# Transposed group totals ahead of matrix products on TensorE, and a later place for some gate products

## The reference, cut to what matters

```
u, gate = split(x @ W_in.T)                 # 2 x 2048 channels
u     = silu(causal_conv4(u) + conv_b)
dt, B, C = split(u @ Wx.T)                  # 64, 16, 16; each rms-normed
delta = softplus(dt @ Wdt.T + dt_bias)
state = exp(delta*A) * state + (delta*u) * B          # for each of 16 states, over time
y     = sum over states of state * C, + u * D_param
x1    = layernorm(x + (y * silu(gate)) @ W_out.T)
out   = layernorm(x1 + x1 @ W.T + b + the LoRA product of the best rank)
```

## Time and profile before

| | |
|---|---|
| median of 3 runs (range) | 2567.99 us (2561.28 to 2569.66) |
| the profiled execution | 2566.21 us, span 2564.4 us |
| PE busy | 2198.9 us, 86% |
| DVE busy | 2140.0 us, 83% |
| POOL busy | 1797.0 us, 70% |
| ACT busy | 1473.6 us, 57% |
| mean granted clock of PE | 0.92 |
| DMA | 353.52 MB, mean 138 GB/s |

### The profile page before, as it was taken

How to read it: one execution, slowest core, us unless ns; L and a number is a source line. 1 busy time by engine, 2 the same in 40 slices (tenths; PEclk the granted TensorE clock), 3 DMA queues, 4 the chain that set the end, 5 groups by cost and what they waited for, 6 DMA issues and landing times.

```text
span 2564.4 us, 30651 instructions
## 1 busy us (share of the span) xinstructions
PE 2198.9 (86%) x10528; PEld 1600.0 (62%) x10528; DVE 2140.0 (83%) x2551; ACT 1473.6 (57%) x2083; POOL 1797.0 (70%) x768
## 2 busy tenths in 40 slices
PE   6988679788879969899979979899979995988977
PEld 5766557577645547687855547677866563765545
DVE  3448789999999499889989789999989789999831
ACT  3368757576655265666675445665675456555421
POOL 3368989888598378777668666877678687678600
PEclk9999889998879979999989989999989996988988
DMA  4265556465223325755542323555453331352213
GB/s 158 63 214 199 185 175 211 151 203 178 78 70 102 104 77 175 253 187 189 169 132 85 103 62 127 187 192 185 156 161 105 103 95 56 131 169 79 78 50 115
DMA packets 152651, 353.52 MB, mean 138 GB/s; under 512 B 17776, under 2 KB 27376, under 8 KB 152496
## 3 DMA queue, kind: packets, MB, share of 16 engines
q1 hardware_dynamic: 152496, 351.56, 42.9%
HBM read 282.65 MB, written 68.85 MB: 137 GB/s over the span
## 4 chain that ended last, share of the span: by engine, by line
PE 54%; DVE 29%; issue 8%; ACT 5%; POOL 3%; DMA 1%; SPq 0%; DVEq 0%; POOLq 0%; ACTq 0%
PE bank L717 15%; DVE drive L796 13%; PE state_t L670 12%; PE bank L694 7%; PE bank L696 7%; PE bank L695 7%; DVE y_acc L811 6%; PE bank L670 3%; DVE scratch L818 2%; PE bank L752 2%; DVE ln_stats L882 1%; POOL drive L1176 1%; ACT decay L1022 1%; ACT L1022 1%; DVE dt_slot L844 1%
## 5 line engine op out<-in xcount | busy, mean ns | idle before, releaser
L1176 POOL TENSOR_TENSOR drive<-delta_u,b_bcast 128x2048 f32<-128x2048 f32 x256 | 1170.7, 4576 | 281.0 <-PE state_t L670 280.3
L796 DVE TENSOR_TENSOR_SCAN drive<-decay,drive 128x512 f32<-128x512 f32 x1024 | 1195.9, 1206 | 53.1 <-POOL drive L1176 33.4
L1022 ACT ACTIVATE decay<-delta,a_sb 128x512 f32<-128x512 f32 x1024 | 693.8, 687 | 397.9 <-DVE drive L796 393.9
L670 PE MATMUL state_t<-identity,drive 128*128 128x128 f32 x4096 | 639.4, 297 | 223.1 <-DVE drive L796 139.0
L670 PEld LDWEIGHTS state_t<-identity,drive 128*128 128x128 f32 x4096 | 514.8, 152 | 438.9 <-DVE drive L796 186.9
L694 PE MATMUL bank<-cols_high,w_split 128*128 128x512 f32 (+1 forms) x1312 | 562.7, 429 | 38.5 <-POOL w_split L1202 37.5
L811 DVE SCALAR_TENSOR_TENSOR y_acc<-state_t,c_rows,y_acc 128x512 f32<-128x512 f32 x720 | 514.9, 737 | 70.3 <-PE state_t L670 65.2
L696 PE MATMUL bank<-cols_high,w_split 128*128 128x512 f32 (+1 forms) x1312 | 526.6, 401 | 0.0
L695 PE MATMUL bank<-cols_low,w_split 128*128 128x512 f32 (+1 forms) x1312 | 524.9, 400 | 0.0
L717 PE MATMUL bank<-channels,w_raw 128*128 128x512 f32 x1024 | 476.5, 596 | 4.6 <-POOL channels L1198 4.6
L1182 POOL TENSOR_TENSOR y_acc<-y_acc,scaled 128x512 f32<-128x512 f32 x240 | 309.7, 1290 | 77.8 <-ACT scaled L1036 77.7
(11 more groups left out here) (92 smaller groups left out, 1396.2 us busy)
## 6 DMA issues: line engine op xcount, KB each, us to landing
w_split<-w_split SPq DMA_DIRECT2D x288, 512.0 KB, 3.7
b_bcast<-b_rows SPq DMA_DIRECT2D x256, 256.0 KB, 3.4
w_raw<-in_w_out SPq DMA_DIRECT2D x128, 256.0 KB, 2.9
w_raw<-in_w_in SPq DMA_DIRECT2D x96, 256.0 KB, 3.5
gates<-scratch SPq DMA_DIRECT2D x64, 256.0 KB, 3.7
scratch<-gates SPq DMA_DIRECT2D x64, 256.0 KB, 4.6
w_raw<-in_x_cols SPq DMA_DIRECT2D x32, 256.0 KB, 3.6
rows<-in_x_rows SPq DMA_DIRECT2D x4, 2048.0 KB, 9.1
```

The lines of the kernel that those rows point to most:

```text
L670: last = engine.transpose(bank[0:tile.shape[1], i * P:(i + 1) * P], tile, identity[:, :])
L796: engine.tensor_tensor_scan(state, decay[(GT * s + t) % DECAYS][:, :], state, 0.0, ALU.mult, ALU.add).then_inc(signal["scan"])
L1022: engine.activation(decay[i % DECAYS][:, :], delta[:, g % 2, t, :], ACT.Exp, scale=a_sb[:, j, n:n + 1]).then_inc(signal["decay"])
L1176: engine.tensor_tensor(drive[key % DRIVES][:, :, :], du[:, :, :], row, ALU.mult).then_inc(signal["drive"])
```

## The change

Two edits to the planning, none to the instructions themselves. The due of `y_turn` is lowered by `TURN_FIRST`, as that of `turn` is. And the number of gate jobs that are listed between the u jobs of the next sequence is no longer `GATES_BEFORE` but `GATES_BEFORE - GATES_LAST`; the last `GATES_LAST` of them are listed after the first two delta jobs (the line that does so, L354, was there and served sequence 0 alone). Between the u jobs of sequences 0 to 3 there were 0, 12, 12 and 8 gate jobs, and now there are 0, 12, 6 and 0. After the delta jobs there were 4, 0, 0 and 0, and now there are 4, 0, 6 and 4. For sequence 3 four more (4 to 7) go from the list of `beside(2)` to the head of that of `beside(3)`, ahead of the out products.

```diff
-GATES_BEFORE = (4, 12, 12, 8)
+GATES_BEFORE = (4, 12, 12, 4)
+
+GATES_LAST = (4, 0, 6, 4)
...
-        put("PE", due, 0.45, "y_turn", key, [("add", (last, tt)) for tt in range(ADDED)] + [("sum", last)],
+        put("PE", due - TURN_FIRST, 0.45, "y_turn", key, [("add", (last, tt)) for tt in range(ADDED)] + [("sum", last)],
             take=[("bank", ("y_turn", key))])
...
-            gates = GATES_BEFORE[b + 1] if b >= 0 else 0
+            gates = GATES_BEFORE[b + 1] - GATES_LAST[b + 1]
```

## The result

| | before | after |
|---|---|---|
| median (range, runs) | 2564.64 us (2552.38 to 2569.66, 4) | 2468.64 us (2466.84 to 2483.21, 4) |
| ratio, 95% interval | | 0.9645 [0.9594, 0.9696] |
| span of the profiled execution | 2564.4 us | 2466.1 us |

96 us came where 63 were forecast: 2469 us lies 34 under the forecast and 9 under the low end of the range. The direction was right and the size was not.

What follows compares the result with a forecast made beforehand. DVE was taken as the bound most of the time, its idle time as what could be won. 55 + 9 + 2 - 3 = 63 us off the profiled 2566.2 gave 2503 us, range 2478 to 2556.

Steps and rivals of the forecast that it cites:

- the 2 us named: First group's end in sequences 1 to 3: first transpose of `y_acc` within some 2 us of the last sum.
- the clock rule: Out products broken up by turns: pauses halve PE's clock, costing up to 18 us; nothing was charged.
- rival D: Out products hold the banks, y_turns don't get through, 34 us come back: 2532 us; chance 0.07.
- the 7.8 that I left: DVE's waits for L863's transposes outside the three holes, `y_turn` waiting for a bank: 7.8 us expected to remain.
- rival B: Matrix chain takes over: the next sequence starts when it did, so the scans' lead is mostly lost: 2550 us; chance 0.17.
- 55 + 4.6 + 2 = 61.6 us: Gains: 55 from sequences 1 and 2's holes, 4.6 from turns in the last sequence, 2 at other groups' ends.
- The factor 0.93: Sequences 1 and 2: DVE turns only 93% of the returned 36.1 + 22.9 us into work, giving 55 us.
- 525.3 of 564 us: Sequence 1 without the holes: DVE's busy time stays 525.3 us in a stretch of 564 us, 93%.
- 4.6 us were counted as won: Last sequence: the wait of 4.63 us for the last y_gate was to go.
- 3 as lost to uncovered gates: Behind sequence 1's out products: four gates of sequence 2 take 21.8 us, 18.6 covered by PE's pause, 3 not.
- rival C: Gates behind the out products delay `x1_turn` because PE's pause closes: 2577 to 2604, say 2590 us; chance 0.10.
- the first term of the sum: DVE holes at the first group's end in sequences 1 and 2: (36.1 + 22.9) x 0.93 = 55 us won.

Runs made afterwards that it cites:

- y_only: The kernel after with the old gate places, so only the lower due of `y_turn` against the kernel before: 2491.4 us, ratio 0.9734.
- y_gates2: Lower due of `y_turn`, six gates of sequence 2 behind its deltas, sequence 3's gates as in the kernel before: 2497.2 us, ratio 0.9747.
- y_gates3: Lower due of `y_turn`, sequence 3's gates moved as in the change, sequence 2's as in the kernel before: 2498.6 us, ratio 0.9757.
- after_again: The kernel after, unchanged, run once more for a second profile: 2470.2 us, ratio 0.9654 to the kernel before.
- gates_only: The kernel after with the old due of `y_turn`, so only the gates moved against the kernel before: 2529.7 us, ratio 0.9888.
- before_again: The kernel before, unchanged, run once more for a second profile: 2561.1 us over 11 runs.
- y_gates_66_00: The kernel after with no gates between the u jobs of sequences 2 and 3, six of sequence 2 behind its deltas: 2490.7 us, ratio 0.9720.
- 8_4: The kernel after, but sequence 3 keeps four gates between its u jobs and four behind its deltas: 2491.1 us, ratio 0.9720.
- 8_8: The kernel after, but all eight early gates of sequence 3 follow its deltas: 2480.4 us, ratio 0.9685.
- drive_in_4: The kernel after with each POOL drive of 128x2048 issued as four of 128x512: 2512.51 us, ratio 0.9831.

## Why the prediction was off

**What held.** The holes were where the rows of before had them and went whole: lags of 0.8, 0.2 and 0.7 us, within the 2 us named. The out products of sequence 0 take 162 us and not 144, 18 more where 17 were worked out. The granted clock in them is 1.00, so charging nothing for the clock rule was right: the turns did not make products dearer. The y_turns got their bank (rival D fell): what DVE waits for them in the whole span, once 22.5 us in 12 waits, is now

```profile
  PE bank L672: 7.5, 7
```

against the 7.8 that I left. The gates were needed as an enabling step: without them at both handovers the time is 21 to 28 us longer by medians (y_only, y_gates2 and y_gates3 against after_again), rival B in part. In the kernel after the chain is early by a few us: POOL's last product for sequence 2's first drive ends at 1260.2, and that drive starts at 1264.4, released by turns of sequence 1.

**What failed, by the terms of the sum.** I count from the first scan of sequence 1 on, with the two profiles of each kernel averaged. Sequences 1 to 3 became 46.3, 33.2 and 12.9 us shorter, 92.4 in all, and the rest of the span 3.4 longer: 89.0 where the sum had 63.

- *The idle time returned.* Of the sum 55 + 4.6 + 2 = 61.6 us are time of DVE in the three sequences; its idle time there fell by 73.6 (166.3 to 92.7), by sequence 39, 27 and 7.5. The stretches of four units that hold the holes went from 37.5, 25.4 and 18.4 us of idle time to 1.1, 0.0 and 1.4. The rest of sequences 1 and 2 became 4 us less idle, that of sequence 3 9.5 more, spread over it; the sum had put only 4.6 us on its hole, and 7.5 came. The factor 0.93, by which DVE was to lose part of the first two holes, was wrong: 66 us came where they had 59. gates_only shows that the gates, which I priced at nothing beside enabling, can give something of their own: 31 us, with 14 us less of lag (88.7 before, 74.9 with it). 12 us too little.
- *The term that wasn't there.* DVE's busy time in the three sequences fell by 18.8 us, which I held constant (525.3 of 564 us). This is the largest error. Some 15 us of it are small instructions that wait for POOL inside their own duration. Over their shortest, counted from 0.45 us, these take 49.4 and 52.8 us in the two profiles of before and 35.7 and 36.3 in those of after. In the first profile of before scans and adds also show 2 ns longer each, 3.3 us over the whole span; the second doesn't show it.
- *Behind the last scan.* 4.6 us were counted as won, PE's wait for the last `y_gate`, and 3 as lost to uncovered gates. The wait is still there:

```profile
2332.07 8.08 PE L719 MATMUL bank<-channels,w_raw 128*128 128x512 f32 x12 [4.23 <-POOL channels L1200]
```

The transposes ahead of it were hardly late before (a lag of 0.1 us), so there was nothing in this wait for a lower due to win. The rest behind the last scan has 11 matmuls more than before and is 3.4 us longer. The 3 us were charged for another place, gates of sequence 2; in the last sequence, where nothing was charged, the cover was gone (rival C's mechanism) and `x1_turn` ends 272 us behind the first scan and not 265. That 3 and 3.4 agree is luck. In all 5 us too much.

63 + 12 + 18.8 - 5 = 89, within rounding. The spans differ by 98.3 because the first scan of sequence 1 also came 9.3 us earlier in this pair of executions. That part isn't of the change: all engines have the same lists up to the first group's end of sequence 1, and before_again shows 718.2 us. The medians over more runs differ by 91, those of the result by 96.

The failed step is thus the first term of the sum, 55 us, worked out with DVE's busy time as a constant and with 0.93 of the holes returned. In its place DVE's busy time fell by 18.8 us and its idle time by 12 more than counted. No rival covers it. Whether the waits on POOL fell for a reason or by chance of alignment I can only argue: 35.7 and 36.3 us repeat within one kernel, and over the variants they go up to 60 us with no order in the edits (59.7 in y_gates_66_00, 51.6 in 8_4, 45.0 in 8_8, 38.6 in y_gates3, 47.7 in gates_only). Each edit shifts where small instructions fall on drives. Of the 21 us between 8_4 and the change, 16 are of this kind. In such a kernel a difference of 10 us between two schedules need not come from what the edit was for.

## What to carry to other kernels

A piece that is ready and gates the next unit of the bound engine needs a due that says so: at three places 2 us of transposes held DVE for 74 us in all. A lead won in one stage is kept only if the chain into every following stage is early too; parts of a change are tested together and alone, since here neither half of the gates' move gained anything without the other. And a forecast that holds an engine's busy time fixed while its instructions shift against another engine's leaves out a term, here 19 us.

## What the runs showed of the hardware

Some small DVE instructions whose operands all lie in SBUF wait inside their recorded duration while POOL works. In the kernels before and after, those that took over 0.3 us more than the shortest of their kind (37 and 35) each ended at most 0.42 us behind the end of a POOL instruction. In the kernel before, POOL's drive and DVE's L935 (two instructions, alone 0.4 us together):

```profile
1292.92 4.64 POOL L1176 TENSOR_TENSOR drive<-delta_u,b_bcast 128x2048 f32<-128x2048 f32 x1 [0.95 <-PE state_t L670]
...
1292.99 4.78 DVE L935 TENSOR_SCALAR twice_rows<-narrow,ssm_rstd 128x64 f32<-128x64 f32 x2
```

The first of the pair took 4.61 us and ended 0.05 us behind the drive. L844 waited longer still, 9.38 us for work that takes 0.42 elsewhere, first DVE, then POOL:

```profile
495.50 9.38 DVE L844 TENSOR_TENSOR dt_slot<-w_raw,dt_slot 64x256 fp32r<-64x256 f32 x1
...
495.20 1.28 POOL L1182 TENSOR_TENSOR y_acc<-y_acc,scaled 128x512 f32<-128x512 f32 x1
496.43 4.51 POOL L1176 TENSOR_TENSOR drive<-delta_u,b_bcast 128x2048 f32<-128x2048 f32 x1
500.88 1.27 POOL L1182 TENSOR_TENSOR y_acc<-y_acc,scaled 128x512 f32<-128x512 f32 x1
502.10 2.50 POOL L1202 TENSOR_TENSOR w_split<-w_raw,w_split 128x512 fp32r<-128x512 f32 x2
```

In the kernel after the same instruction found a pause:

```profile
494.25 1.29 DVE L846 TENSOR_TENSOR dt_slot<-w_raw,dt_slot 64x256 fp32r<-64x256 f32 x1
```

Up to the first scan of sequence 1, 13 of the profiles are of the same lists. In six this instruction took 9.4 us and sequence 0 548.5 to 555.9 us, 550.6 on average; in seven it took 1.3 us and sequence 0 542.1 to 549.0, 545.1 on average. On average 5.5 of the 8.1 us thus arrive. Which of the two comes goes by execution and not by kernel: after_again has 9.41 us.

The Trainium skill (SBUF — State Buffer, SBUF: two separate sides) describes one port pair that DVE and GpSimd share as an exclusive lock: a DVE instruction with two inputs in SBUF (against a GpSimd instruction that reads SBUF) or in a two-port mode, and any GpSimd instruction, get it for the whole instruction, whichever starts first, while "the other fully blocks". The trace agrees that the waiter blocks to the end of a POOL instruction. It agrees on the scans too, which have one input in SBUF (`drive`) and one in PSUM (`decay`, L485) and are not held. In the kernel before 756 of them ran wholly while POOL was busy and took 1205 ns on average, and 110 ran with POOL idle and took 1207. The extremes of all 1024 in the kernel after (ns: min/median/max), beside those of a kind that is held:

```profile
L798 DVE TENSOR_TENSOR_SCAN drive<-decay,drive x1024: 1168/1208/1225, 171.8 to 2317.4; 128x512 f32<-128x512 f32 x171
...
L937 DVE TENSOR_SCALAR twice_rows<-narrow,ssm_rstd x32: 241/246/4684, 142.1 to 1783.6; 128x64 f32<-128x64 f32 x32
```

L935 (L937 here) has one large input in SBUF; whether it ran in a two-port mode no trace shows. What the trace shows beyond this is that the waiter can lose to a row of POOL instructions that start after it (four here, eight in drive_in_4 behind 504.61). Scans are what DVE mostly does, and the two engines are busy 86% and 73% of the span side by side. What lets some waiters in after one POOL instruction and not others stays open, and so does whether the kernel would gain the whole of the 15 us if they were kept apart.
